# A two-layer spectral block on one core: channel-major filter temporaries, a regrouped prologue, reordered seams around the MLP, and products on constants in TensorE's waits

## The chip, the core and the metric

The kernel runs on one core of one Trainium2 chip. The metric is the device time of one execution in microseconds (us), lower is better. TensorE (PE) multiplies, VectorE (DVE), ScalarE (ACT) and GpSimd (POOL) do the elementwise work, SyncE (SP) issues nearly all transfers. All data are float32.

## What is computed

Two layers act on x of shape 2 x 128 x 128 x 128 (image, height, width, channel). Each layer does:

```python
residual = x
h = layer_norm(x, n1_g, n1_b)
h = afno_filter(h, w1, b1, w2, b2) + residual
residual = h
h = layer_norm(h, n2_g, n2_b)
h = gelu(h @ mw1 + mb1)       # exact, 128 -> 512
return h @ mw2 + mb2 + residual
# afno_filter(x):
xf = rfft2(x, norm='ortho')                    # over height and width
o1 = relu(block_diagonal(xf, w1) + b1)         # complex, 8 blocks of 16 channels
o2 = softshrink(block_diagonal(o1, w2) + b2, 0.01)
return irfft2(o2, norm='ortho') + x
```

## The kernel before

**Steps and stages.** A step is one layer on one image, four in all (`STEPS`, step 2 is the change of layer). A tile is four image rows, there are 32. On the partitions lies the width (or, inside the transform, a frequency or a channel pair). Each step has these stages, in the order of the main loop of TensorE (L686 to L693):
- `dft_w` (L486): the transform along the width, 32 groups of four channels, products at L496. ScalarE and VectorE evict alternate groups to SBUF (`a_out`, the copy at L336).
- `filter_` (L554): 34 units, 32 of them for four frequencies of one half of the channels, two small ones for the last frequency. For a unit: transform along the height (`dft_h`, L506), copy by ScalarE (`g_copy`, L708), first block product (`mix1`, L521/L523), `e_copy` by ScalarE, two combining operations of VectorE (`combine`, L931 and L932), `o_relu` by ScalarE (L722), second block product (`mix2`, L550), and on VectorE `shrink`: v = product + bias (L942), cl = clamp(v) (L944), v - cl written into the arena (L959). TensorE takes the units staggered: `dft_h(n+2)`, `mix1(n+1)`, `mix2(n)`. v and cl lie frequency-major; the arena wants the frequencies of a channel side by side, so L959 writes with 128 words from one channel to the next, channel innermost.
- `idft_h` (L581): the inverse along the height, 32 groups of four channels at L590, evicted alternately by ScalarE and VectorE (`evict_v`, L363).
- `mlp` (L646): the inverse along the width for two tiles at a time (first pair L654, others `idft_w`, L607 and L613), sums with the residual on VectorE (`h2`, L1007 to L1018), layer norm statistics (L879) and the inverse deviation in twelve small operations (`inverse_std`, L313 to L322, and L1127), normalizing on ScalarE (L737), transposes on TensorE (`turn`, L621), splitting of the tile in a high and a low part (L745 on ScalarE, `lower`, L1024, on VectorE), `fc1` (L632 to L634), gelu (L751), `fc2` (L641), and the new x on VectorE (`x_new`, L1038, `last_tile`, L1047), which SyncE stores.

**The next image beside the MLP.** While TensorE does the MLP of one step, the other engines prepare the next: SyncE loads `xnext`, VectorE takes its statistics, GpSimd normalizes four rows a tile into the other arena (`z_rows`, L1191; these are the scalings), multiplies the result by the gain (L1160), adds `mb2` to the residual of the current step (L1198) and adds xnext (L1164), and SyncE puts the sum `aside` in DRAM until the next step reads it. The next `dft_w` waits for all 32 tiles of `z_new`.

**The prologue of step 0.** It does that job with nothing beside it: four loads of 8 tiles, for each batch statistics and inverse deviation on VectorE (L879 to L899), and then scalings by ScalarE (22 of 32 tiles, L762) and VectorE (10 tiles, L904), gain product and residual on GpSimd (24 tiles, L1160 and L1164 of the loop at L1168) as soon as a tile is normalized, and on VectorE (8 tiles, L921 and L923, between the evictions of dft_w). The filter of step 0 overwrites the first 13 tiles of `first`, so ScalarE waits for their stores (`early_st`, L778).

**Weights of a layer.** `build_spectral` (L846) masks the block weights into dense matrices by 24 products of VectorE (L862), waits for two small products of TensorE (`dc_bias`, L475, L482), and scales (L871). For layer 1 it runs at the end of step 1's MLP, and `dc_bias(1)` stands before `dft_w(2)` in TensorE's queue. `split_weights` (L987) splits `mw1` in two parts after the first pair.

All waits are on semaphores by hand; an engine executes its queue in order, so an instruction that waits holds all behind it.

## Time and profile before

| quantity | us |
|---|---|
| median of 3 runs | 1789.91 |
| lowest and highest | 1786.05, 1791.61 |
| the profiled execution | 1787.48 |
| its span (first to last instruction) | 1785.7 |

| engine | busy us | share of the span |
|---|---|---|
| TensorE products | 1636.1 | 92% |
| TensorE weight loads (beside products) | 1453.6 | 81% |
| VectorE | 1195.5 | 67% |
| ScalarE | 934.6 | 52% |
| GpSimd | 630.5 | 35% |

The mean granted TensorE clock is 0.977 of full speed. A busy share is an average over stages: which engine ends a stage last has to be read stage by stage. All further times of a row are us from the start of the span, durations in us unless ns is said.

### The profile page before, as it was taken

To read this page: it belongs to the slowest core of one execution; us is meant where nothing else is said; L and a number is where in the kernel's file an instruction comes from. 1 tells how busy PE (TensorE), PEld (TensorE's weight loads), DVE (VectorE), ACT (ScalarE), POOL (GpSimd) and SP (SyncE) were. 2 spreads that over 40 slices of the span, in tenths; PEclk is the share of its full clock that TensorE was granted. 3 is DMA by queue.
4 is the path that set the end of the run, shared out by engine and by line. 5 is a ranking of instruction groups with operands and counts; after the bars stand their busy time and mean duration, and the time that the engine had idled before them with its cause. 6 is when DMAs were issued, how large, how long until landed. Compare 5 with 4: busy or idle time off the path is not lost.

```text
span 1785.7 us, 35087 instructions
## 1 busy us (share of the span) xinstructions
PE 1636.1 (92%) x11184; PEld 1453.6 (81%) x11184; DVE 1195.5 (67%) x2880; ACT 934.6 (52%) x1778; POOL 630.5 (35%) x756
## 2 busy tenths in 40 slices
PE   0099989999999998999999998999999999899999
PEld 0088878888889887888889887888888988688888
DVE  7959956666646976666664895666664697566663
ACT  4335426666634534666652452666663453466665
POOL 4800004777750001677781000477775000111111
PEclk9999989999998998999998999999999999999999
DMA  8210061333320033333330006133332003211111
GB/s 246 100 54 1 1 220 59 101 105 105 100 80 1 1 115 117 103 103 106 106 101 24 1 1 220 54 97 103 106 107 84 1 1 126 77 36 31 34 36 48
DMA packets 164896, 138.85 MB, mean 78 GB/s; under 512 B 9186, under 2 KB 127332, under 8 KB 164804
## 3 DMA queue, kind: packets, MB, share of 16 engines
q1 hardware_dynamic: 164516, 137.15, 24.0%
q8 instruction: 58, 0.95, 0.2%
q10 hardware_dynamic: 288, 0.46, 0.1%
q14 instruction: 34, 0.28, 0.0%
HBM read 70.47 MB, written 67.11 MB: 77 GB/s over the span
## 4 chain that ended last, share of the span: by engine, by line
PE 44%; DVE 21%; POOL 17%; issue 15%; ACT 1%; DVEq 1%; DMA 1%; SPq 0%; POOLq 0%; ACTq 0%
PE ps L641 13%; PE ps L496 7%; PE ps L590 6%; POOL arena L1191 6%; POOL gz L1160 4%; DVE vsb L942 4%; POOL gz L1164 4%; PE ps L632 4%; PE ps L634 3%; PE ps L633 3%; DVE csb L944 3%; DVE usb L931 3%; DVE usb L932 2%; POOL arena L1198 2%; PE ps L621 2%
## 5 line engine op out<-in xcount | busy, mean ns | idle before, releaser
L641 PEld LDWEIGHTS ps<-mw,gel 128*128 128x128 f32 x4096 | 533.2, 191 | 43.3
L641 PE MATMUL ps<-mw,gel 128*128 128x128 f32 x4096 | 536.4, 274 | 0.0
L751 ACT ACTIVATE gel<-ps,mb1f 128x512 f32<-128x512 f32 x512 | 351.6, 687 | 269.9 <-PE ps L634 238.7
L1198 POOL TENSOR_TENSOR arena<-arena,mb2rep 128x512 f32<-128x512 f32 x128 | 163.5, 1277 | 886.0 <-ACT hn L737 886.0
L632 PE MATMUL ps<-hth,mw1h 128*128 128x512 f32 x512 | 262.9, 513 | 8.1 <-DVE htl L1024 7.8
L1191 POOL TENSOR_SCALAR arena<-xnext,rstd,shift 128x128 f32<-128x128 f32 x384 | 168.4, 457 | 217.7 <-DVE shift L1127 217.7
L737 ACT ACTIVATE hn<-arena,shift,rstd 128x128 f32 (+1 forms) x512 | 221.6, 482 | 35.6 <-DVE shift L1127 35.6
L1007 DVE TENSOR_TENSOR arena<-ps,arena 128x512 f32 (+1 forms) x64 | 44.2, 691 | 266.0 <-PE ps L613 241.9
L496 PE MATMUL ps<-cst,arena 128*128 128x128 f32 x1024 | 130.2, 294 | 90.3 <-DVE arena L904 81.4
L634 PE MATMUL ps<-hth,mw1l 128*128 128x512 f32 x512 | 204.4, 399 | 0.0
L496 PEld LDWEIGHTS ps<-cst,arena 128*128 128x128 f32 x1024 | 129.4, 208 | 90.8 <-DVE arena L904 81.5
L633 PE MATMUL ps<-htl,mw1h 128*128 128x512 f32 x512 | 203.2, 397 | 0.0
L722 ACT ACTIVATE osb<-usb,vectors 128x512 f32<-128x512 f32 (+1 forms) x136 | 95.6, 703 | 172.2 <-DVE usb L932 172.2
L550 PEld LDWEIGHTS ps<-w2s,osb 128*128 128x128 f32 x1040 | 131.2, 195 | 46.0 <-ACT osb L722 44.0
L550 PE MATMUL ps<-w2s,osb 128*128 128x128 f32 x1040 | 153.9, 291 | 11.8 <-ACT osb L722 11.2
L959 DVE TENSOR_TENSOR arena<-vsb,csb 128x512 f32 (+2 forms) x128 | 133.6, 1044 | 15.4 <-DVE csb L944 0.2
L506 PE MATMUL ps<-cst,arena 128*128 128x128 f32 x1024 | 138.9, 280 | 0.3
L506 PEld LDWEIGHTS ps<-cst,arena 128*128 128x128 f32 x1024 | 128.3, 196 | 1.2 <-issue 0.8
L1160 POOL TENSOR_TENSOR gz<-arena,gain 128x512 f32<-128x512 f32 x96 | 124.6, 1298 | 8.0
L1024 DVE TENSOR_TENSOR htl<-ps,hth 128x512 fp32r<-128x512 f32 x128 | 88.2, 689 | 57.0 <-ACT hth L745 56.9
L1164 POOL TENSOR_TENSOR gz<-xnext,gz 128x512 f32<-128x512 f32 x96 | 122.4, 1275 | 0.5
L632 PEld LDWEIGHTS ps<-hth,mw1h 128*128 128x128 f32 x512 | 99.5, 194 | 24.3 <-issue 21.2
(92 smaller groups left out, 2428.8 us busy)
## 6 DMA issues: line engine op xcount, KB each, us to landing
arena<-aside SPq DMA_DIRECT2D x128, 256.0 KB, 5.0
aside<-gz SPq DMA_DIRECT2D x96, 256.0 KB, 3.0
between<-xout SPq DMA_DIRECT2D x62, 256.0 KB, 2.3
xnext<-between SPq DMA_DIRECT2D x62, 256.0 KB, 3.0
out_dram<-xout SPq DMA_DIRECT2D x62, 256.0 KB, 2.3
aside<-first SPq DMA_DIRECT2D x32, 256.0 KB, 2.0
xnext<-in_x_dram SPq DMA_DIRECT2D x31, 256.0 KB, 3.0
mw1raw<-in_L_mw_dram SPq DMA_DIRECT2D x4, 256.0 KB, 2.5
```

Of the source, the lines that this page charges most:

```text
L496: mm = pe.matmul(ps[:, 2 + cg % 4, P * i:P * i + P], rows_of(s)[:, (GROUP * cg + i) // 2, :, i % 2], FW, start=True, stop=True)
L506: mm = pe.matmul(ps[:, q, P * i:P * i + P], spec_of(s)[:, GROUP * b + i, q].rearrange("p r c -> p (r c)"), FH, start=True, stop=True)
L550: mm = pe.matmul(ps[:, 4 + q, P * i:P * i + P], osb[:, q, i, :], w2s[:, q].rearrange("p r c -> p (r c)"), start=True, stop=True)
L632: pe.matmul(bank, h, hth[:, r % 2, :], start=True, stop=False)
L633: pe.matmul(bank, h, htl[:, r % 2, :], start=False, stop=False)
L634: pe.matmul(bank, l, hth[:, r % 2, :], start=False, stop=True).then_inc(f1_mm, 1)
L641: mm = pe.matmul(ps[:, r % 2, P * i:P * i + P], gel[:, r % 2, m, P * i:P * i + P], mw2[:, m, :], start=(m == 0 and i == 0), stop=(m == CHU ...
L737: ins = act.activation(hn[:, r % 2, i, :], row, ACT.Identity, bias=shift[:, r // 2, r % 2 * ROWS + i:r % 2 * ROWS + i + 1], scale=rstd[:, ...
L751: act.activation(gel[:, r % 2, m, :], ps[:, 2 + m % 2], ACT.Gelu, bias=mb1f[:, m:m + 1]).then_inc(gelu_out, 1)
L1160: pool.tensor_tensor(by_row(tmp), ztile(s, h0), gains(gain1[:, :]), ALU.mult).then_inc(gz_done, 1)
L1191: ins = pool.tensor_scalar(zrow(s + 1, h0 + k), pairs(xnext[:, r, k, :]), rstd[:, r // 2, row:row + 1], shift[:, r // 2, row:row + 1], ALU ...
L1198: pool.tensor_tensor(t, t, b, ALU.add).then_inc(mb2_done, 1)
```

## The change

In the prologue the batches are 4, 8, 8, 8 and 4 tiles, the first load stands before the parameter loads, GpSimd takes part in the scalings (15 tiles, ScalarE 15, VectorE 2), and all gain products and residuals follow the last scaling: 12 tiles on GpSimd, 20 on VectorE with their temporaries in PSUM. ScalarE evicts all of dft_w of step 0. The building of the weights is moved behind the first batch, and for layer 1 between the evictions of dft_w of step 2; `dc_bias(1)` follows that dft_w. The filter's temporaries are channel-major. The last four groups of idft_h are evicted by ScalarE; the first pair's inverse along the width is done in two pieces, channels 0 to 95 inside idft_h and the rest after it, its sums likewise, and `split_weights` is done within idft_h. TensorE runs 14 and 5 products of two constant matrices, whose result nobody reads, before and after the first transposes. At the end of the MLP VectorE takes the last statistics before an earlier `x_new`, and GpSimd does the last scalings before the gain products.

```diff
-PRO_ACT = (7, 6, 6, 3)
+BATCH = (4, 8, 8, 8, 4)
+PRO_POOL = (2, 4, 4, 4, 1)
+PRO_ACT = (2, 4, 4, 4, 1)
-R_DVE = 8
+R_DVE = 20
+PARTS = 12
+SOON = 24
+V_DVE = SOON // 2 + 2
+V_ACT = CGROUPS - V_DVE
-Z_DVE0 = TILES - sum(PRO_ACT)
+Z_DVE0 = TILES - sum(PRO_ACT) - sum(PRO_POOL)
...
+        b2cols = sb("b2cols", [P, 2, HALF, 2])
-        vsb = at("vsb", [P, 2, GROUP, 2, HALF], o); o += size(vsb.shape)
-        csb = at("csb", [P, 2, GROUP, 2, HALF], o); o += size(csb.shape)
+        vsb = at("vsb", [P, 2, HALF, GROUP, 2], o); o += size(vsb.shape)
+        csb = at("csb", [P, 2, HALF, GROUP, 2], o); o += size(csb.shape)
...
+            for b in range(len(BATCH)):
+                lo, hi = at_row[b], at_row[b + 1]
+                if lo <= HALF < hi:
+                    load_first(b, lo, HALF - lo, lo + 1)
+                    sp.dma_start(first[:, HALF, :], source[0][0]).then_inc(row0_in, 16)
+                    load_first(b, HALF + 1, hi - HALF - 1, HALF + 1)
+                else:
+                    load_first(b, lo, hi - lo, lo + (lo < HALF))
+                if b == 0:
+                    load_spectral(0)
+                    load_gain(0)
...
-            for t in range(TILES):
+            turns = sorted(range(TILES), key=lambda t: 2 * t + 1 if t < R_POOL0 else t - R_POOL0)
+            for t in turns:
...
                     for r in range(4):
                         store(TILES // 4 - 1, r)
+                    for r in range(4):
                         put_aside(s, TILES // 4 - 1, r)
...
+            def first_pair(s, a, b):
+                if a == 0:
+                    pe.wait_ge(h2_done, TILES * s)
+                for cg in (b - 2, b - 1):
+                    turned(s, cg)
+                t = slice(GROUP // 2 * a, GROUP // 2 * b)
+                for bank, m, h0 in ((6, DE, 0), (7, DO, H - ROWS)):
+                    dst = ps[:, bank - (2 if a else 0), 0:ROWS * GROUP * (b - a)]
+                    mm = pe.matmul(dst, m, v_of(s)[:, t, h0:h0 + ROWS, :], start=True, stop=True)
+                mm.then_inc(iw_soon if a == 0 else iw_mm, 1)
...
                     mm.then_inc(ih_mm, 1)
+                    if cg == SOON + 1:
+                        first_pair(s, 0, SOON)
...
+            def keep_warm(n):
+                for _ in range(n):
+                    pe.matmul(ps[:, 2, 0:P], IDENT, FH, start=True, stop=True)
+
             def mlp(s):
-                pe.wait_ge(h2_done, TILES * s)
-                for half in range(2):
...
+                turned(s, SOON + 3)
+                first_pair(s, SOON, CGROUPS)
                 mlp_bias(s)
                 idft_w(s, 1)
+                keep_warm(14)
                 turn(s, 0, 0)
+                keep_warm(5)
                 pe.wait_ge(mlp_w, s + 1)
...
-                if s % IMAGES == 0:
+                if s == 0:
+                    dc_bias(0)
+                dft_w(s)
+                if s and s % IMAGES == 0:
                     dc_bias(s // IMAGES)
-                dft_w(s)
...
-                        for r in (0, 2):
+                        for r in ((0, 2) if s else range(4)):
                             a_out(s, q, j, r)
...
-                with act.Fori(0, CGROUPS // 4) as j:
+                with act.Fori(0, SOON // 4) as j:
                     for r in (0, 2):
                         v_out_(s, 4 * j + r, r)
+                for cg in (SOON, SOON + 2, *range(SOON + 4, CGROUPS)):
+                    v_out_(s, cg, cg % 4)
...
+                if b == 0:
+                    build_spectral(0)
+                if b == 1:
+                    scale_spectral(0)
+                for t in range(t0 + PRO_POOL[b], t0 + BATCH[b] - PRO_ACT[b]):
...
-                own.add(dve.tensor_tensor(by_row(gz0[:, :, :]), ztile(0, ROWS * t), gains(gain1[:, :]), ALU.mult))
+                tmp = ps[:, 6].rearrange("p (h c) -> p h c", h=ROWS)
+                own.add(dve.tensor_tensor(by_row(tmp), ztile(0, ROWS * t), gains(ps[:, 7, C:2 * C]), ALU.mult))
                 own.settle()
-                dve.tensor_tensor(first[:, h, :], first[:, h, :], gz0[:, :, :], ALU.add).then_inc(r_dve, 1)
+                dve.tensor_tensor(first[:, h, :], first[:, h, :], tmp, ALU.add).then_inc(r_dve, 1)
...
-                bias = b2rep[:, q].rearrange("p r c -> p (r c)").unsqueeze(1).to_broadcast([P, kws, P])
-                v = vsb[:, q].rearrange("p j r c -> p j (r c)")[:, 0:kws]
-                cl = csb[:, q].rearrange("p j r c -> p j (r c)")[:, 0:kws]
-                src = ps[:, 4 + q, 0:P * kws].rearrange("p (j k) -> p j k", j=kws)
+                bias = b2cols[:, q].unsqueeze(2).to_broadcast([P, HALF, kws, 2])
+                v, cl = vsb[:, q, :, 0:kws], csb[:, q, :, 0:kws]
+                src = ps[:, 4 + q, 0:P * kws].rearrange("p (j r c) -> p c j r", j=kws, r=2)
                 dve.tensor_tensor(v, src, bias, ALU.add).then_inc(v_out, 1)
...
-                dst = dst.rearrange("p c k -> p k c")
-                v, cl = (t.rearrange("p j r c -> p (j r) c") for t in (v, cl))
+                v, cl = (t.rearrange("p c j r -> p c (j r)") for t in (v, cl))
                 dve.tensor_tensor(dst, v, cl, ALU.subtract).then_inc(y_done, 1)
...
+                elif s % IMAGES:
...
+                else:
+                    dve.wait_ge(spec_in, SPEC_IN * (s // IMAGES + 1))
+                    for cg in range(1, CGROUPS, 2):
+                        a_out(s, 2 * cg // CGROUPS, cg % (CGROUPS // 2) // 4, cg % 4)
+                        if cg // 2 < PARTS:
+                            build_part(cg // 2)
+                        if cg // 2 == PARTS:
+                            build_done()
+                    scale_spectral(s // IMAGES)
...
+                split_weights(s)
+                dve.wait_ge(resid_in[0], RESID_IN[0] * (s + 1))
+                v_out_(s, SOON + 1, 1)
+                dve.wait_ge(iw_soon, s + 1)
+                h2_evens(s, 0, SOON)
+                v_out_(s, SOON + 3, 3)
+                own.settle()
+                h2_odds(s, 0, SOON)
+                own.settle()
...
-                    if known >= 3:
+                    if 3 <= known <= PAIRS or last and known > PAIRS:
                         x_new(s, i + (2 * h - 5) // 4, (2 * h - 5) % 4)
...
+                    if known > PAIRS and not last:
+                        x_new(s, i + (2 * h - 5) // 4, (2 * h - 5) % 4)
...
+            for b in range(len(BATCH)):
+                pool.wait_ge(st_pro, b + 1)
+                for t in range(sum(BATCH[:b]), sum(BATCH[:b]) + PRO_POOL[b]):
...
+                j = TILES // 4 - 1
+                if not last:
+                    ready(j, 0)
+                    z_rows(j, 0)
+                    z_rows(j, 1)
+                for n in (TILES - 2, TILES - 1):
+                    biased(n)
+                if not last:
+                    ready(j, 2)
+                    z_rows(j, 2)
+                    z_rows(j, 3)
+                    scaled(j, 0)
```

`turned(s, cg)` and `evicted(s, cg)` are waits for the eviction of group cg, by the engine that now does it; `h2_evens` and `h2_odds` are the two halves of `h2` on a range of channels; `ready`, `scaled`, `added`, `biased` are GpSimd's old pieces (wait for the statistics, gain product, residual, mb2).

## Rows read from the trace of the kernel before

**Rows 1.** Busy time per stage; columns: stretch, its length, the engines' busy time (instructions), granted clock, DMA.
```profile
core 0: us, PE busy (x) PEld busy (x) DVE busy (x) ACT busy (x) POOL busy (x), PEclk, DMA share, GB/s
0.00:91.90 91.90, 0.98 (x5) 0.92 (x5) 81.03 (x182) 35.59 (x89) 60.47 (x52) 1.00 0.54 168
...
126.00:223.40 97.40, 93.38 (x652) 82.06 (x653) 86.85 (x174) 49.75 (x102) 0.00 (x0) 0.99 0.02 6
223.40:252.80 29.40, 29.40 (x258) 29.40 (x257) 12.54 (x18) 9.30 (x16) 0.00 (x0) 0.97 0.89 308
252.80:272.40 19.60, 12.32 (x44) 7.98 (x44) 15.53 (x46) 8.27 (x17) 2.55 (x2) 0.74 0.12 40
272.40:509.60 237.20, 237.20 (x1573) 207.83 (x1571) 151.50 (x430) 148.67 (x274) 166.90 (x214) 1.00 0.32 98
```

**Rows 2.** Order of time, prologue; columns: start, duration, engine, line, output<-inputs, count, wait.
```profile
2.75 0.84 SPq L390 DMA_DIRECT2D first<-in_x_dram  x1
...
5.33 2.62 DVE L862 TENSOR_TENSOR w1s<-wraw,cst 64x64 f32<-64x64 f32 x16 [5.33 <-DMA betarow<-in_L_n_b_dram]
...
13.51 5.38 DVE L879 BATCH_NORM_STATS2 pst<-first 128x6 f32<-128x256 f32 x16 [1.82 <-DMA first<-in_x_dram]
...
21.67 10.89 ACT L762 ACTIVATE arena<-first,pnm,prs 128x128 f32<-128x128 f32 x28 [18.70 <-DVEq L900]
...
30.74 1.25 POOL L1160 TENSOR_TENSOR xout<-arena,gain 128x512 f32<-128x512 f32 x1
30.86 1.18 DVE L320 TENSOR_TENSOR pn<-pn,pva 128x32 f32<-128x32 f32 x1
```

**Rows 3.** Order of time, dft_w of step 0 and the first copy of its filter.
```profile
91.90 31.82 PEld L496 LDWEIGHTS ps<-cst,arena 128*128 128x128 f32 x256 [81.52 <-DVE arena L904]
...
123.94 0.69 DVE L336 COPY arena<-ps 128x512 f32<-128x512 f32 x1 [1.15 <-PE ps L496]
...
126.04 0.26 ACT L705 COPY nyq<-ps 64x128 f32<-64x128 f32 x1 [2.34 <-DVE first L923]
```

**Rows 4.** Groups by line and shape, filter of step 0 (150 to 214): busy us, mean ns.
```profile
L959 DVE TENSOR_TENSOR arena<-vsb,csb 128x512 f32 x23 | 24.4, 1060 | 3.3
...
L942 DVE TENSOR_TENSOR vsb<-ps,b2rep 128x512 f32<-128x512 f32 x23 | 15.7, 683 | 0.0
...
L944 DVE TENSOR_SCALAR csb<-vsb 128x512 f32<-128x512 f32 x23 | 9.8, 427 | 0.8
```

**Rows 5.** Order of time, filter of step 0: weight loads of dft_h, and L959.
```profile
146.61 0.97 PEld L506 LDWEIGHTS ps<-cst,arena 128*128 128x128 f32 x8
...
154.56 0.97 PEld L506 LDWEIGHTS ps<-cst,arena 128*128 128x128 f32 x8
...
182.40 1.05 DVE L959 TENSOR_TENSOR arena<-vsb,csb 128x512 f32 x1
...
216.40 1.06 DVE L959 TENSOR_TENSOR arena<-vsb,csb 128x512 f32 x1
```

**Rows 6.** Order of time, end of the MLP of step 0 and start of dft_w of step 1.
```profile
502.80 0.19 DVE L320 TENSOR_TENSOR nt<-nt,var 128x8 f32<-128x8 f32 x1
...
505.47 1.20 DVE L1127 SCALAR_TENSOR_TENSOR shift<-stats,rstd 128x8 f32<-128x8 f32 x1
...
512.26 1.74 POOL L1191 TENSOR_SCALAR arena<-xnext,rstd,shift 128x128 f32<-128x128 f32 x4
...
514.05 2.29 PE L496 MATMUL ps<-cst,arena 128*128 128x128 f32 x9 [4.43 <-POOL arena L1191]
```

**Rows 7.** Order of time, start of the MLP of step 0.
```profile
252.86 2.27 PE L654 MATMUL ps<-arena,cst 128*128 128x256 f32 x8
...
257.88 1.43 DVE L879 BATCH_NORM_STATS2 stats<-arena 128x6 f32<-128x256 f32 x4
...
263.46 1.12 PE L621 MATMUL ps<-cst,hn 128*128 128x128 f32 x4 [3.14 <-ACT hn L737]
...
266.24 0.77 PE L632 MATMUL ps<-hth,mw1h 128*128 128x512 f32 x1 [1.67 <-DVE htl L1024]
```

**Rows 8.** Order of time, TensorE between the MLP of step 1 and dft_w of step 2.
```profile
939.75 1.01 PE L482 MATMUL ps<-vectors,w1s 64*128 64x1 f32 x4 [4.94 <-DVEq L864]
```

More of the change, by code:

```diff
@@ L209, in afno @@
         nt0 = sb("nt0", [P, 4 * ROWS])
-        gz0 = sb("gz0", [P, ROWS, C])
         xout_at = top[0]
@@ L1221, in _, with ready, scaled @@
-                for n in range(TILES + 4):
-                    tile(n // 4, n % 4)
+                def ready(j, r):
+                    pool.wait_ge(rs_done, RS * s + 2 * (j + 1) + r // 2 + 1)
+                def scaled(j, r):
+                    m = 4 * j + r
+                    pool.wait_ge(z_new, TILES * s + m + 1)
+                    if s or m >= 4:
+                        pool.wait_ge(gz_st[r], 16 * (TILES // 4 * s + j))
+                    scale(s + 1, ROWS * tile_of(j, r), gz[:, r])
@@ new lines, in added, with biased @@
+                def added(j, r):
+                    pool.wait_ge(gz_done, R_POOL0 + TILES * s + 4 * j + r + 1)
+                    residual(gz[:, r], xnext[:, r], gz[:, r])
+                def biased(n):
+                    pool.wait_ge(hn_done, TILES * s + n + 1)
+                    bias(s, n // 4, n % 4)
+                for n in range(TILES):
+                    j, r = n // 4 - 1, n % 4
+                    if j >= 0 and not last:
+                        ready(j, r)
+                        z_rows(j, r)
+                        scaled(j, r)
+                    if n >= 2:
+                        biased(n - 2)
+                    if j >= 0 and not last:
+                        added(j, r)
```

207 lines of the change are left out of this document (109 added, 98 removed).

## Prediction

> **What bounds the kernel now.** I read the busy time by stage first, then the instructions in order of time at each seam between stages. One step (there are four, one per layer and image) is five stages: dft_w, filter, idft_h, the start of the MLP, the MLP. In the MLP TensorE is busy for all of its 237.20 us and in the filter for 93.38 of 97.40, with VectorE at 86.85 beside it; in the first 91.90 us TensorE does 0.98 us of work [rows 1]. So the change has to be read at three kinds of place: the prologue, where VectorE sets the pace; the filter, where two engines are close to each other; and the seams, where TensorE idles.
>
> The prologue's chain: statistics begin at 13.51, when the first load has landed; those of a batch of eight tiles take 5.38, and the twelve small operations of the inverse deviation take 2.78 when GpSimd is idle (18.89 to ScalarE's start at 21.67), so 0.23 each. Once GpSimd multiplies and adds, one of them takes 1.18, about as long as the GpSimd operation beside it (1.25) [rows 2]. dft_w starts at 91.90 and the filter's first copy at 126.04, after a wait of 2.34 for the last VectorE residual [rows 3].
>
> **Prologue.** After: batches of 4, 8, 8, 8, 4 tiles; GpSimd and ScalarE normalize 15 tiles each and VectorE two; all gain products and residuals come after the last normalized row. First load: half the bytes and first in its queue. Before, 2 MB took 10.76 from its issue at 2.75; half is 5.4, plus the issue and the constants that share the engines; I take 8.0 (bounds 6 and 10). VectorE then has 4 tiles of statistics 2.7 and 2.8 of small operations (13.5), the 24 products that build the weights (16 take 2.62, so 4.0, plus a copy 0.3: 17.8), then 8.2 for each of three batches (with 1.3 for scaling the weights in the first) to 43.7, 5.5 for the last to 49.2. I add 0.9 for the products that run beside GpSimd's scalings: 50.1. GpSimd normalizes a tile in 1.74 [rows 6]: four tiles from 44.6 end at 51.6, the last at 53.3. ScalarE takes 10.89/7 = 1.56 a tile [rows 2]: 44.6 + 6.2 + 1.6 = 52.4. VectorE's two tiles hide beside these. dft_w starts at 53.4: 38.5 earlier.
> What had been hidden under the prologue now lies beside dft_w, 31.8 long [rows 3]: GpSimd does 12 tiles of two operations, 12 x 2 x 1.3 = 31.2, ending at 84.6; the store of that tile has to land (about 2) before ScalarE may write over it, so 86.8. VectorE does 20 tiles of two operations with one operand in PSUM, 20 x 1.44 = 29, ending near 83 (nearest row the eviction L336 of the same size, 0.69 [rows 3]; a write to PSUM by VectorE is not in the trace; between 0.69 and the 1.06 of L959 [rows 4], with which it would be 37 and end at 91). ScalarE takes all 32 evictions: at 9.30/16 = 0.58 each [rows 1] they fit into 31.8. The filter's first copy comes at 86.8 against 126.04: I take a gain of 39 (bounds 34 and 42). If GpSimd blocked VectorE in its scalings as it does in its products, each small operation would take up to 1.74/4 = 0.44; the one row with a scaling beside it shows 0.19 [rows 6], so I don't charge it.
> The Trainium skill ("SBUF — State Buffer", the section on the bandwidth-pool intuition) says that GpSimd and a two-port VectorE operation exclude each other entirely. The products agree with it and the scalings do not; charged in full for the two batches whose small operations meet a scaling, twelve times 0.2 each, it is an estimate of 5 us more, 1712.
>
> **Filter.** The temporaries v and cl change from frequency-major to channel-major, so the last of the three operations of shrink (L959) writes runs of eight words instead of single words 512 B apart. It takes 1.060 now [rows 4] against 0.69 for the eviction L336, which writes 512 elements in runs of four [rows 3]; new value 0.69. The add (L942, 0.683 [rows 4]) now reads PSUM with a stride; L336 also does, 512 B from word to word, so I leave it (bounds 0.68 and 1.06). The clamp (L944, 0.427 [rows 4]) stays contiguous. VectorE's time per unit was (216.40 - 182.40)/12 = 2.83 [rows 5] and becomes 2.46. But TensorE needs (154.56 - 146.61)/3 = 2.65 per unit where it waits for nothing [rows 5]. So a unit gains 2.83 - 2.65 = 0.18 and no more. In step 0 TensorE's pace holds up to 154.56; from there to the last but two units before 216.40 [rows 5] there are (214 - 154.56)/2.83 = 21 units: 3.8. The last three units have less TensorE work and keep VectorE's whole 0.37: 1.1. Together, rounded, 5.0 per step, 20 for four (bounds 0 and 24).
>
> **Start of the MLP.** Three quarters of the first pair of row products move into idft_h: about 1.45 of TensorE time is spent earlier, and idft_h ends that much later. Against that, ScalarE evicts the last four column groups (0.58 each), and after the last there remain only products of 128 columns (0.45) and four short VectorE sums (1.2). Sum after the old end of idft_h: 1.45 + 0.75 + 0.45 + 0.2 + 1.3 = 4.15, against 257.88 - 252.86 = 5.0 before [rows 7]. The weight split moves into idft_h, where VectorE is busy for 12.54 of 29.40 [rows 1], so it is hidden there; without that cover it would cost its two operations of 512 elements, about 1.3. Queued behind the new wait for iw_soon are two evictions' worth of VectorE work; TensorE needs the first only four groups later. Then the chain statistics, normalize, transpose, copy, subtract. The transposes took 1.12 and fc1 started at 266.24 [rows 7]; the granted clock of this stretch is 0.74 [rows 1], so both levels, 1.2 and 2.4 GHz, occur in it, and TensorE had been waiting before each. The 14 + 5 products on constants take 29.40/128 = 0.23 each at the upper level [rows 1]: 3.2 after the second pair of row products, ending some 0.5 before the normalized tile is there, and 1.1 in the wait for htl. With TensorE at the upper level the transposes and the first fc1 group save 0.5 each, and VectorE's h2 no longer stands before the subtraction (0.2). In all 0.8 + 0.5 + 0.5 + 0.2 + 0.2 for later fc1 groups = 2.2 per step, 8.8 in all (bounds 2 and 12).
>
> **End of the MLP.** TensorE starts dft_w of step 1 at 514.05, after GpSimd's last scaling (512.26 + 1.74), and had waited 4.43, so it had finished at 509.62 [rows 6]. GpSimd now does the last two tiles' scalings before their gain products, and VectorE does the statistics before the x of an earlier tile. The statistics end by 504.9 instead of 506.67 (L1127 at 505.47 alone took 1.20 beside a product [rows 6]); then 2 x 1.75: 508.5. TensorE's own end is then last: gain 4.3 for steps 0 and 2. At the change of layer TensorE waited 4.94 for the built weights and with the bias products (1.01) began dft_w 5.8 after its MLP [rows 8]; the building moves between evictions, where VectorE waits 1.15 before each [rows 3], against two products of 0.16: 5.8. Total 14.4 (bounds 8 and 16). The x of tile 29 is now ready only 0.3 before fc2 of tile 31 asks for it; if it is later, it costs that. The bias product and the scaling of the weights now follow dft_w at that one place: 1.0 lost. Without the idle gap dft_w starts at the upper clock; its first groups of steps 1 to 3 ran below it: 2 gained (0 to 4).
> The DMAs that change place (the weights of step 0 behind the first batch, stores of step 0 in another order, the last asides behind the last x stores) stand behind nothing that is needed sooner: the last aside is read a whole dft_w later.
>
> **Sum.** 39 + 20 + 8.8 + 14.4 + 2 - 1 = 83.2. The profiled execution took 1787.5 (span 1785.7); its median is 2.4 more. 1787.5 - 83.2 = 1704.3, and 1706.7 in terms of the median.
>
> **Rivals.**
> (a) The filter gains nothing: L959 keeps 1.06 because the channels still lie 512 B apart. For it: no row has this mix of run and stride. Against: L336 [rows 3] also writes short runs, at 0.69. 1707 + 20 = 1727.
> (b) Slower than before: reading PSUM in channel order costs L942 what L959's writes cost now (0.38 more), the clamp falls to one element a cycle (0.27 more), and L959 doesn't gain. A unit is then 3.48, 128 units lose 83, the rest gains 63: 1787.5 + 20 + 2.4 = 1810. It decides from 0.49 more per unit (3.32) on. Against it is L336 at 0.69 with a strided read of PSUM [rows 3].
> The Trainium skill ("SBUF — State Buffer", the section on the DMA port swizzle) says that PSUM has lines of 8 bytes and that reads that are not contiguous are slow; it says so of matmuls. L336 shows no such price for VectorE; L959 shows one, for writes to SBUF.
> (c) The products on constants backfire: TensorE falls to the lower level anyway, 14 of them take twice as long, 6.4, and the transposes wait for them 2.9 longer than before, in four steps 11.5 lost instead of 8.8 gained: 1727.
> (d) The last scalings still come late (the statistics wait for GpSimd's biases or for the loads): half of the seams' gain goes, 1714.
> (e) The prologue is paced by something else (VectorE beside GpSimd's scalings, or the load): 5 to 6 us, 1712.
>
> **Chances.** Forecast 0.60; (a) 0.12; (b) 0.03; (c) 0.10; (d) 0.06; (e) 0.09. Range: the forecast's own bounds (filter +4, prologue +3, start +3, others +3 on the good side; as much again on the bad one) give 1692 to 1722; with (a) and (c) 1690 to 1730. A difference under 0.3% (5 us) can't be told from no change. Faster 0.96, same 0.01, slower 0.03.
>
> **What would show it.** dft_w starts at 53 (right: 51 to 57). L959's successor takes 0.69 and L942's 0.69; filter units follow each other at 2.65, and VectorE then waits, not TensorE. fc1 starts some 11.9 after the old end of idft_h (13.4 before) and its products are at the upper clock. TensorE's wait before dft_w is under 0.5. It would be wrong most by a filter unit at 2.83 or more, or by a first filter copy after 92.

## The result and the profile after

The changed kernel takes 1695.8 us (median of four, 1691.4 to 1697.6) against 1788.1 for the kernel before on the same chip: ratio 0.948, 95% interval 0.945 to 0.950. The forecast was 1706.7. The gain is 92 where the prediction had 83. The profiled execution took 1697.6 with a span of 1695.9 and a mean granted clock of 0.996 (0.977 before).

To see where the time went I lay the first instructions of the stages on TensorE side by side, each stage from its own first instruction to the first one of the next (us; worked out from the two traces):

| | before, step 0 | 1 | 2 | 3 | after, step 0 | 1 | 2 | 3 |
|---|---|---|---|---|---|---|---|---|
| start of dft_w | 91.9 | 514.1 | 940.7 | 1365.9 | 54.9 | 463.3 | 869.6 | 1285.8 |
| dft_w | 31.7 | 32.2 | 32.3 | 32.9 | 31.6 | 30.2 | **35.6** | 30.2 |
| filter | 99.6 | 102.9 | 102.9 | 98.4 | 93.7 | 93.0 | **96.6** | 93.0 |
| idft_h | 29.6 | 28.7 | 28.7 | 28.7 | 30.0 | 30.0 | 30.9 | 30.0 |
| its end to fc2 | 19.6 | 19.8 | 19.8 | 19.2 | 16.2 | 16.2 | 16.2 | 16.2 |
| MLP from fc2 on | 237.0 | 237.0 | 237.0 | 237.0 | 237.0 | 237.0 | 237.0 | 237.0 |
| idle until the next dft_w | 4.6 | 6.1 | 4.6 | | 0 | 0 | 0 | |

The differences: prologue 37.0, dft_w 1.7, filters 27.3, idft_h with the start of the MLP 8.3, idle at the seams 15.5: 89.8, the difference of the two spans. Step 1 of the changed kernel, which nothing disturbs, takes 406.3 to the next dft_w; step 2 is longer by 9.9, which the prediction had not foreseen.

**Prologue.** The changed kernel in order of time, the lines that answer to [rows 2] and [rows 3]:

```profile
8.61 2.73 DVE L943 BATCH_NORM_STATS2 pst<-first 128x6 f32<-128x256 f32 x8 [8.61 <-DMA first<-in_x_dram]
...
43.06 0.38 DVE L326 TENSOR_TENSOR pn<-prs 128x32 f32<-128x32 f32 x1
43.48 0.38 DVE L328 TENSOR_TENSOR pn<-pn,pva 128x32 f32<-128x32 f32 x1
43.89 0.19 DVE L330 SCALAR_TENSOR_TENSOR prs<-pn,prs 128x32 f32<-128x32 f32 x1
...
45.77 9.06 POOL L1280 TENSOR_SCALAR arena<-first,prs,pnm 128x128 f32<-128x128 f32 x20 [1.52 <-DVE pnm L961]
...
54.94 1.36 PEld L524 LDWEIGHTS ps<-cst,arena 128*128 128x128 f32 x6 [35.29 <-issue]
...
88.46 0.26 ACT L757 COPY nyq<-ps 64x128 f32<-64x128 f32 x1 [0.94 <-DMA aside<-first]
```

The first load landed at 8.61. A small operation of VectorE beside a scaling of GpSimd mostly takes 0.17 to 0.20, now and then 0.25 to 0.49 (0.38 at 43.06), against 1.18 beside a gain product before. GpSimd's last five tiles end at 54.83 and release dft_w. The filter's first copy waits 0.94 for a store to land, no longer for VectorE.

**Filter.** The groups by line and shape in the filter of step 0 (110 to 174), which answer to [rows 4]; and one round of weight loads, which answers to [rows 5]:

```profile
L1011 DVE TENSOR_TENSOR vsb<-ps,b2cols 128x512 f32<-128x512 f32 x25 | 17.1, 682 | 0.0
L1026 DVE TENSOR_TENSOR arena<-vsb,csb 128x512 f32 x24 | 16.6, 693 | 3.4
L1013 DVE TENSOR_SCALAR csb<-vsb 128x512 f32<-128x512 f32 x25 | 10.7, 427 | 0.9
```
```profile
130.19 0.97 PEld L534 LDWEIGHTS ps<-cst,arena 128*128 128x128 f32 x8
...
132.84 0.97 PEld L534 LDWEIGHTS ps<-cst,arena 128*128 128x128 f32 x8
```

The write into the arena (L1026, the former L959) takes 693 ns instead of 1060, the add that now reads PSUM with a stride stays at 682, the clamp at 427. A unit follows every 2.65, TensorE's own pace.

**Start of the MLP.** TensorE in step 0, in order of time (compare [rows 7]):

```profile
214.41 0.19 PEld L700 LDWEIGHTS ps<-cst 128*128 128x128 f32 x1 [0.24 <-issue]
214.84 3.09 PEld L700 LDWEIGHTS ps<-cst 128*128 128x128 f32 x27 [0.24 <-issue]
218.63 0.42 PEld L672 LDWEIGHTS ps<-cst,hn 128*128 128x128 f32 x4 [0.69 <-ACT hn L789]
219.02 1.20 PEld L700 LDWEIGHTS ps<-cst 128*128 128x128 f32 x10
220.75 0.19 PEld L683 LDWEIGHTS ps<-hth,mw1h 128*128 128x128 f32 x1 [0.54 <-issue]
```

A product on constants appears as two rows, so 14 are 28. They end 0.69 before the normalized tile is there. fc1 comes 10.6 after the end of idft_h, which itself is 1.3 longer: 11.9 after the old end.

**Seams.** GpSimd and TensorE at the end of step 0, which answer to [rows 6]:

```profile
458.82 3.48 POOL L1307 TENSOR_SCALAR arena<-xnext,rstd,shift 128x128 f32<-128x128 f32 x8 [2.15 <-DVE shift L1238]
462.26 2.53 POOL L1269 TENSOR_TENSOR gz<-arena,gain 128x512 f32<-128x512 f32 x2
```
```profile
460.83 2.73 PE L692 MATMUL ps<-mw,gel 128*128 128x128 f32 x23
463.40 2.87 PE L524 MATMUL ps<-cst,arena 128*128 128x128 f32 x23
```

The last scaling ends at 462.30, one microsecond before TensorE wants it, and dft_w follows the MLP without a gap.

**The clock.** Busy time of stretches; columns: stretch, length, the engines' busy time (instructions), granted clock, DMA share, GB/s. The first two are of the kernel before (filters of steps 1 and 2), the next two of the changed kernel:

```profile
552.90:563.10 10.20, 10.20 (x43) 9.32 (x42) 6.05 (x17) 3.12 (x7) 0.00 (x0) 0.50 0.00 0
979.50:989.80 10.30, 10.30 (x43) 9.43 (x43) 6.12 (x17) 3.12 (x7) 0.00 (x0) 0.50 0.01 2
```
```profile
493.40:586.50 93.10, 90.85 (x672) 85.21 (x671) 81.51 (x175) 53.06 (x103) 0.00 (x0) 1.00 0.00 1
616.40:632.60 16.20, 12.55 (x78) 10.03 (x78) 12.27 (x43) 8.39 (x17) 2.57 (x2) 1.00 0.24 89
```

Before, TensorE ran at the lower of its levels (0.50 of full speed) for a part of every step, 82 us in all; after, only in three stretches of step 2, 13.7 us together. The start of the MLP is at 1.00 where it was at 0.74 [rows 1].

**The stall in step 2.** Between the evictions of this dft_w stand VectorE's products for the new layer's weights. VectorE, GpSimd and TensorE of the changed kernel:

```profile
872.48 6.20 DVE L919 TENSOR_TENSOR w1s<-wraw,cst 64x64 f32<-64x64 f32 x2
878.61 0.67 DVE L344 COPY arena<-ps 128x512 f32<-128x512 f32 x1
879.21 0.34 DVE L919 TENSOR_TENSOR w1s<-wraw,cst 64x64 f32<-64x64 f32 x2
```
```profile
872.27 1.27 POOL L1269 TENSOR_TENSOR gz<-arena,gain 128x512 f32<-128x512 f32 x1
873.50 1.27 POOL L1273 TENSOR_TENSOR gz<-xnext,gz 128x512 f32<-128x512 f32 x1
874.73 1.29 POOL L1269 TENSOR_TENSOR gz<-arena,gain 128x512 f32<-128x512 f32 x1
875.97 2.49 POOL L1273 TENSOR_TENSOR gz<-xnext,gz 128x512 f32<-128x512 f32 x2
```
```profile
879.34 5.92 PE L524 MATMUL ps<-cst,arena 128*128 128x128 f32 x35 [2.89 <-DVE arena L344]
```

Two products that take 0.34 elsewhere take 6.20, beside the last five operations of an unbroken run of two-operand operations on GpSimd: they end 0.2 after that run (878.46). An eviction stands behind them, and TensorE waits 2.89 for it.

### The profile page after: what moved, and what is told of

Same layout as the page of the kernel before. It is cut to its first block, busy times and chain, and to the rows that moved or that the text cites. A ratio compares the mean times of both kernels' runs of the same rounds, so it can differ in the third digit from the quotient of the medians.

```text
span 1695.9 us, 35295 instructions
## 1 busy us (share of the span) xinstructions
PE 1611.5 (95%) x11336; PEld 1458.9 (86%) x11336; DVE 1136.1 (67%) x2879; ACT 949.7 (56%) x1774; POOL 628.3 (37%) x792
## 4 chain that ended last, share of the span: by engine, by line
PE 88%; DVE 4%; POOL 2%; ACT 2%; issue 1%; DMA 0%; DVEq 0%; ACTq 0%
PE ps L692 27%; PE ps L683 7%; PE ps L685 7%; PE ps L639 7%; PE ps L684 7%; PE ps L578 7%; PE ps L534 6%; PE ps L524 5%; PE ps L549 3%; PE ps L672 3%; PE ps L551 3%; PE ps L658 3%; PE ps L664 3%; POOL first L1273 1%; POOL xout L1269 1%; DVE stats L943 1%
## 5 line engine op out<-in xcount | busy, mean ns | idle before, releaser
L524 PE MATMUL ps<-cst,arena 128*128 128x128 f32 x1024 | 124.6, 286 | 38.1 <-POOL arena L1280 35.2
L524 PEld LDWEIGHTS ps<-cst,arena 128*128 128x128 f32 x1024 | 124.0, 200 | 38.4 <-issue 35.3
L578 PEld LDWEIGHTS ps<-w2s,osb 128*128 128x128 f32 x1040 | 137.4, 194 | 18.9 <-ACT osb L774 13.2
L578 PE MATMUL ps<-w2s,osb 128*128 128x128 f32 x1040 | 142.9, 280 | 8.5 <-ACT osb L774 7.9
L534 PE MATMUL ps<-cst,arena 128*128 128x128 f32 x1024 | 136.2, 276 | 0.2
L534 PEld LDWEIGHTS ps<-cst,arena 128*128 128x128 f32 x1024 | 125.7, 193 | 0.9 <-issue 0.5
L797 ACT CAST hth<-ps 128x512 fp32r<-128x512 f32 x128 | 75.2, 588 | 79.7 <-PE ps L672 79.7
```

Of the source, the lines that this page charges most:

```text
L524: mm = pe.matmul(ps[:, 2 + cg % 4, P * i:P * i + P], rows_of(s)[:, (GROUP * cg + i) // 2, :, i % 2], FW, start=True, stop=True)
L534: mm = pe.matmul(ps[:, q, P * i:P * i + P], spec_of(s)[:, GROUP * b + i, q].rearrange("p r c -> p (r c)"), FH, start=True, stop=True)
L578: mm = pe.matmul(ps[:, 4 + q, P * i:P * i + P], osb[:, q, i, :], w2s[:, q].rearrange("p r c -> p (r c)"), start=True, stop=True)
```

## The experiments

Each ran with the kernel before beside it on the same chip. A change of a few microseconds is read from the stages of the trace, since executions of one kernel differ by up to 11 with the share of time at the lower clock: the changed kernel took 1691.5 where its mean granted clock was 1.000, and 1697.9 where it was 0.995. "Longer than the changed kernel" is said against its first median, 1695.8; the medians of the kernel before lay between 1785.4 and 1788.6 in these groups of runs, so a few microseconds of such a difference mean nothing.

**The layout by itself, taken away and added.** First the changed kernel with the old order of v and cl:

```diff
-        vsb = at("vsb", [P, 2, HALF, GROUP, 2], o); o += size(vsb.shape)
-        csb = at("csb", [P, 2, HALF, GROUP, 2], o); o += size(csb.shape)
+        vsb = at("vsb", [P, 2, GROUP, 2, HALF], o); o += size(vsb.shape)
+        csb = at("csb", [P, 2, GROUP, 2, HALF], o); o += size(csb.shape)
...
-                v, cl = (t.rearrange("p c j r -> p c (j r)") for t in (v, cl))
+                dst = dst.rearrange("p c k -> p k c")
+                v, cl = (t.rearrange("p j r c -> p (j r) c") for t in (v, cl))
```

> The changed kernel with the filter's temporaries frequency-major again; everything else stays. Theory (VectorE paces the old filter at 2.83 us a unit, TensorE the new one at 2.65): units come 2.83 apart again, the last operation of shrink takes 1.06 again, each of the four filters is 5 to 6 us longer, and the kernel takes 1696 + 22 = 1718. Rival (the layout is worth all that the filter stages gained between the two kernels, 27 us): 1723 or more. Rival (the layout is worth nothing, the filters gained by the seams alone): 1696.

1720.9 (1715.0 to 1725.7), ratio to before 0.962 [0.959, 0.966]: 25 longer than the changed kernel, between the 1718 of the theory and the 1723 of the first rival. The filters of steps 1 to 3 take 98.30 each, where an undisturbed one of the changed kernel takes 93.03, 5.3 a filter or 21 in all; the last operation is back at its old time:

```profile
L1029 DVE TENSOR_TENSOR arena<-vsb,csb 128x512 f32 x19 | 20.1, 1060 | 2.7
```

Then the kernel before with the channel-major layout and nothing else of the change (the bias copied once into that order; the buffer gz0 gave way to a temporary in PSUM):

> The kernel before with channel-major temporaries and the transposed copy of the bias, nothing else of the change (to make room in SBUF the eight residual temporaries of VectorE lie in PSUM, as in the changed kernel). Theory: units 2.65 apart, each filter 5 to 6 us shorter, 1788 - 22 = 1766; the stretches at the lower clock at the start of the filters of steps 1 and 2 stay, because the idle gap before dft_w stays. Rival (the layout is worth 27 us): 1761. Rival (VectorE was not the pace of the old filter): 1788.

1766.1 (1763.9 to 1771.6), ratio 0.988 [0.985, 0.991]: 21.6 shorter than before. The operation takes 693 ns here too, a filter 93.0 where no stretch at the lower clock falls into it (step 2) and up to 97.7 where one does (step 3). So the layout is worth 21 by its units and 22 to 25 in the medians whatever stands around it, and rival (a) is out. One part of the expectation failed: the idle time before dft_w stayed, but the stretches at the lower clock did not stay at the start of the filters of steps 1 and 2; the one of 10 us lay at the start of step 3's.

**Which engine paces the filter.** The changed kernel with the clamp done twice (the last two lines of the edit count the added operation):

```diff
-                own.add(dve.tensor_scalar(cl, v, -LAM, LAM, ALU.max, ALU.min))
-                own.settle()
+                for _ in range(2):
+                    own.add(dve.tensor_scalar(cl, v, -LAM, LAM, ALU.max, ALU.min))
+                    own.settle()
...
-                    own.enter(b, 2, 2)
+                    own.enter(b, 4, 2)
```

> The changed kernel with the clamp of each filter unit done twice (the same result): 0.43 us more on VectorE in each of the 32 large units. Theory: TensorE sets the pace of 2.65 us per unit, VectorE needs 2.46 and has 0.19 to spare; the unit becomes 2.46 + 0.43 = 2.89 and each filter 24 to 30 units x 0.24 = 6 to 8 longer, 24 to 30 in all: 1720 to 1726. Rival V (VectorE already paced the filter at 2.65): the unit becomes 3.08, 52 in all, 1748. Rival N (there is more slack than the sum of the rows says): unchanged.

1743.8 (1742.2 to 1746.1): 48 longer than the changed kernel (49 by its second run, on the same chip), 104.3 a filter. The time is nearer to rival V than to the theory, so I read the unit itself, VectorE in order of time:

```profile
120.08 0.41 DVE L1002 TENSOR_TENSOR usb<-usb,ps 128x252 f32<-128x252 f32 x1
120.41 0.68 DVE L1011 TENSOR_TENSOR vsb<-ps,b2cols 128x512 f32<-128x512 f32 x1
121.13 0.89 DVE L1014 TENSOR_SCALAR csb<-vsb 128x512 f32<-128x512 f32 x2
122.16 0.69 DVE L1027 TENSOR_TENSOR arena<-vsb,csb 128x512 f32 x1
122.77 0.41 DVE L1001 TENSOR_TENSOR usb<-usb,ps 128x252 f32<-128x252 f32 x1
123.09 0.41 DVE L1002 TENSOR_TENSOR usb<-usb,ps 128x252 f32<-128x252 f32 x1
```

A unit is now 3.01 and VectorE never waits. The second clamp adds 0.46 (its 0.43 and 0.03 until it starts), so without it VectorE needs 3.01 - 0.46 = 2.55, not 2.46. TensorE still paces the changed filter at 2.65, but by 0.10 and not by 0.19. In the changed kernel itself the next operation starts 0.70 after L1026 does (129.31 to 130.01) where it starts 0.61 after it here (122.16 to 122.77): a wait of 0.09, which agrees. Most of the 0.09 that the forecast of 2.46 lacked was lost in the way durations were subtracted: that distance was 0.90 in the kernel before (154.06 to 154.96), a saving of 0.29, while the printed durations differ by 0.37.

**The prologue: which of its edits carries it.** The kernel before with one wait moved:

```diff
-            done = [0, 0]
+            pool.wait_ge(z_dve, Z_DVE0)
+            pool.wait_ge(z_act, sum(PRO_ACT))
             for t in range(R_POOL0):
-                who = 0 if t % PB < PB - PRO_ACT[t // PB] else 1
-                done[who] += 1
-                pool.wait_ge((z_dve, z_act)[who], done[who])
```

> The kernel before with one wait moved: GpSimd begins its gain products of the prologue only after the last scaling of VectorE and ScalarE. Nothing else of the change. Theory L (the prologue was long because GpSimd's two-operand operations hold up VectorE's, 1.18 instead of 0.19 for a small operation and 8.06 for two tiles of scalings instead of 2.26): VectorE's chain is then 22.9, twice 10.4, and 5.4 + 2.8 + 5.7 for the last batch, and dft_w starts at 57.6 instead of 91.9. GpSimd's 24 tiles then last to 119 and give a part back: the first copy of the filter at 95 instead of 126, and up to 10 lost by VectorE in the filter beside GpSimd. Time 1762 (1755 to 1770). Rival (the chain was long for its own work or the loads): dft_w starts after 85 and the time is 1780 to 1800, since the products come later for nothing.

1792.0 (1788.5 to 1796.1), ratio 1.002 [1.001, 1.003]: nothing gained, and the time is the rival's. The trace shows that the theory's mechanism was there and its consequence was not. VectorE, TensorE, GpSimd and ScalarE, in order of time:

```profile
39.12 0.19 DVE L320 TENSOR_TENSOR pn<-pn,pva 128x32 f32<-128x32 f32 x1
41.27 2.15 DVE L904 TENSOR_SCALAR arena<-first,pst,prs 128x128 f32<-128x128 f32 x8
```
```profile
56.84 5.41 PEld L496 LDWEIGHTS ps<-cst,arena 128*128 128x128 f32 x25 [46.55 <-DVE arena L904]
```
```profile
124.15 1.26 POOL L1164 TENSOR_TENSOR first<-first,xout 128x512 f32<-128x512 f32 x1
```
```profile
125.44 0.26 ACT L705 COPY nyq<-ps 64x128 f32<-64x128 f32 x1 [35.05 <-POOL first L1164]
```

No operation of VectorE is held up before dft_w, which starts at 56.84 (57.6 expected, 91.9 before). But the first copy of the filter comes at 125.44, where it had been at 126.04. I had let it wait for the first 13 tiles; the code waits for all 24 residuals of GpSimd. What the chain gained, the queue of products gave back.

So the other half had to be tried, the changed kernel with GpSimd keeping 24 of these tiles:

```diff
-R_DVE = 20
+R_DVE = 8
```

> The changed kernel with the split of the gain products and residuals of the prologue as before: 24 tiles on GpSimd and 8 on VectorE, instead of 12 and 20. The scalings still come first. Theory C (the prologue's gain needs both edits: scalings first, and half of GpSimd's products given to VectorE): dft_w still starts at 54 to 55, but ScalarE's first filter copy waits for GpSimd's 24 tiles at 2.55 to 2.86 each, that is until 116 to 124 instead of 88; with a stretch at the lower clock after that wait the time is 1724 to 1736. Rival (the split is a detail): under 10 longer than the changed kernel, below 1706.

1729.8 (1728.8 to 1731.6), 34 longer than the changed kernel. dft_w starts at 54.2 and the copy waits:

```profile
116.12 0.26 ACT L757 COPY nyq<-ps 64x128 f32<-64x128 f32 x1 [28.71 <-POOL first L1273]
```

Of the 34, 27.7 are this wait (116.12 against 88.46); the filter behind it starts at the lower clock (0.92 from 118 to 220). The two edits are complements: alone the first is worth nothing, and without the second the changed kernel loses 34. Not tried by themselves: the second edit in the kernel before, the batches of 4 and 8 tiles, and the first load at the head of its queue.

The third part, GpSimd's share in the scalings:

```diff
-PRO_POOL = (2, 4, 4, 4, 1)
-PRO_ACT = (2, 4, 4, 4, 1)
+PRO_POOL = (0, 0, 0, 0, 0)
+PRO_ACT = (3, 6, 6, 6, 2)
```

> The changed kernel with GpSimd's 15 scalings of the prologue given to ScalarE (23 tiles) and VectorE (9). Theory: VectorE's chain gets 7.9 longer (seven tiles of 1.13) less some 0.9 that GpSimd's scalings cost its small operations; the last batch but one is ready at 50.9 instead of 45.8, ScalarE's six tiles of it (9.4) and two of the last (3.1) end at 63.4, and dft_w starts there, 8.5 to 9 later than in the changed kernel: 1703 to 1706. Rival (GpSimd's scalings cost VectorE what they spare it): dft_w starts before 57, 1694 to 1698.

1703.5 (1700.9 to 1708.6), 8 longer. dft_w starts at 61.2 (ScalarE's last scaling ends at 61.15), 6.3 later than in the changed kernel; 8.5 had been expected. GpSimd's scalings are worth their place, though rival (e) had a grain of truth: without them the small operations of VectorE all take 0.19.

**The seams.** The changed kernel with the old order of the last tiles on GpSimd and VectorE:

```diff
...
-                    if known > PAIRS and not last:
-                        x_new(s, i + (2 * h - 5) // 4, (2 * h - 5) % 4)
...
-                for n in range(TILES):
+                for n in range(TILES + 4):
...
-                if not last:
-                    ready(j, 0)
-                    z_rows(j, 0)
-                    z_rows(j, 1)
...
```

> The changed kernel with the old order at the end of the MLP: GpSimd does each tile's gain product before the next tile's scaling, and VectorE writes the x of an earlier tile before the last statistics. Theory: TensorE waits 4.3 to 4.9 for the last scalings at each of the three seams (14 together), and the lower clock comes back at the start of dft_w or of the filter behind them (2 to 4): span 16 to 18 longer, 1712 to 1714. Rival (the order isn't what closed the seams, but something earlier in the MLP): under 5 longer, 1696 to 1701.

1712.6 (1711.8 to 1715.5), 17 longer. The idle time is back at all three seams (5.1 each), and the dft_w behind them take 31.5 to 32.7, where that of step 1 in the changed kernel takes 30.15:

```profile
468.59 1.75 POOL L1305 TENSOR_SCALAR arena<-xnext,rstd,shift 128x128 f32<-128x128 f32 x4
```
```profile
470.39 3.87 PE L524 MATMUL ps<-cst,arena 128*128 128x128 f32 x19 [5.11 <-POOL arena L1305]
```

The stall of step 2 is gone in this run: only two of GpSimd's products stand behind the last scaling, they end at 886.1, and VectorE's first product for the weights comes at 887.71 and takes 0.34 with its neighbour. The new order at the seams and the new place of the weight products make the stall between them.

**The products on constants.** The changed kernel without its two `keep_warm` calls:

> The changed kernel without the 14 and 5 products on constants. Theory: TensorE idles for 3 us before the first transposes and falls to the lower clock around fc1 in each step, as before the change: from the end of idft_h to the first fc2 it takes 1.0 to 2.0 us more than 16.2, in four steps 4 to 8, so 1700 to 1704. Rival (the closed gaps alone keep the upper clock, the products are idle work): 1696, with the granted clock at 1.0 in that stretch. Rival (the products held the transposes up): 1690.

1699.1 (1697.7 to 1700.4), 3.3 longer, just under the 1700 expected; the intervals of the two ratios overlap (0.950 [0.948, 0.952] against 0.948 [0.945, 0.950]), so the gain is read from the stage. The start of the MLP takes 16.7 to 17.4 instead of 16.2, its granted clock is 0.80 instead of 1.00 (stretch of step 1), and 41 us of the kernel lie at the lower clock instead of 13.7. By the stage they pay 3.0 in four steps, where the prediction had 4 (1.0 a step).

**The weights of the new layer.** The changed kernel with their products begun ten evictions later, two parts at a time, when GpSimd has done its run:

```diff
-                        if cg // 2 < PARTS:
-                            build_part(cg // 2)
-                        if cg // 2 == PARTS:
+                        part = 2 * (cg // 2 - 5)
+                        if 0 <= part < PARTS:
+                            build_part(part)
+                            build_part(part + 1)
+                        if part == PARTS:
```

> The changed kernel with the weights of layer 1 built from the sixth eviction of VectorE in dft_w of step 2 on, two parts per eviction, instead of from the first on, one part each: none of the products then runs beside GpSimd's last gain products and residuals. Theory (a VectorE product with two operands in SBUF is kept out while GpSimd's two-operand operations follow each other without a gap: 6.07 us for one product at 872.5; TensorE then waits 2.9 for evictions and falls to the lower clock): dft_w of step 2 takes 30.2 to 31.2 instead of 35.6, the stretches at the lower clock in step 2 are gone, in all 6 to 9 us: 1688 to 1690. Rival (building between evictions is what costs, wherever it stands): 35 again for dft_w of step 2 and 1696.

1696.8 (two others 1693.4 and 1696.7; a fourth execution took 3368.6, which nothing on record explains and which is left out): the same as the changed kernel, not the 1688 to 1690 expected. The stall is gone, four products in 0.62:

```profile
891.48 0.62 DVE L919 TENSOR_TENSOR w1s<-wraw,cst 64x64 f32<-64x64 f32 x4
```

dft_w of step 2 takes 30.9 instead of 35.6 and its filter 93.0 instead of 96.6, 8.3 gained. They are lost again elsewhere: 20.5 us at the lower clock lie in the other three steps, a stretch of 3.4 in each on the constant products. TensorE in step 0:

```profile
215.63 0.33 PEld L700 LDWEIGHTS ps<-cst 128*128 128x128 f32 x1 [0.52 <-issue]
216.48 3.94 PEld L700 LDWEIGHTS ps<-cst 128*128 128x128 f32 x27 [0.52 <-issue]
220.34 0.47 PEld L672 LDWEIGHTS ps<-cst,hn 128*128 128x128 f32 x4
```

The transposes no longer wait for the tile but for the products; the stage is 17.2, as if it had none. This is rival (c) in small: 1.0 a step. So the stage shows what made the stall, and no gain in the whole time came of its removal.

To see whether the stall was an accident I ran the changed kernel a second time:

> The changed kernel, without an edit, a second time. Theory S (the stall in the change of layer is built in: while the weight products stand between the evictions, one VectorE product meets GpSimd's run of two-operand operations in every execution): dft_w of step 2 is again longer than that of steps 1 and 3 (35.57 against 30.15 in the first profile), by 3 to 6 us, and the time is 1695 to 1697. Theory R (it was an accident of one execution): dft_w of step 2 is within 1 us of the others and the profiled span is 1686 to 1691.

1694.7 (1691.5 to 1697.9); dft_w of step 2 took 35.49, with a wait of 2.81 for the same eviction. It is built in. Then both remedies together, the later weights and 9 products instead of 14:

> The changed kernel with the weight products of the new layer begun ten evictions later (as in the run of that name) and 9 instead of 14 products on constants before the first transposes. Theory: when a stretch at the lower clock falls on the 14 products, they last into the transposes and the stage loses 1.0 (17.2 instead of 16.2, three of the four steps there). With 9 the stretch from the end of idft_h to fc2 is 16.2 to 16.5 in all four steps, and the time is 2 to 4 us under that run's 1696.8: 1693 to 1695. Rival: the clock falls more often with fewer products (transposes and first fc1 at the lower level), the start is 16.7 to 17.4 and the time 1697 to 1699.

1695.7 (1689.5 to 1698.6). The start is 16.2 in all four steps although a stretch at the lower clock fell on the products of step 3 (its 18 rows ended before the tile came). The time is still that of the changed kernel within the scatter. The mechanism of the expectation held, its sum didn't show.

At last these two with one more tile of residuals on VectorE (`R_DVE = 21`):

> The changed kernel with three small edits: the new layer's weight products ten evictions later, 9 instead of 14 products on constants, and 21 instead of 20 tiles of the prologue's residuals on VectorE (GpSimd, whose last residual ends at 86.25 in the changed kernel, then ends 2.5 earlier). Theory: the first filter copy comes 0.8 earlier, dft_w of step 2 takes 31 instead of 35.5, and what stretches at the lower clock take elsewhere leaves 1 to 3 of it: 1692 to 1694. Rival K (the stretches at the lower clock take all of it again): 1695 to 1696, the same as the changed kernel.

1691.9 (1688.6 to 1697.7), ratio 0.949 [0.946, 0.951] against 0.950 [0.947, 0.952] for the changed kernel in its second run. The copy of the filter was not earlier (88.55 against 88.46). The profiled execution had no stretch at the lower clock before the last few microseconds and a span of 1686.9, with dft_w of step 2 at 30.9 and all filters at 93.0 to 93.3. Where both kernels ran at a mean clock of 1.000 they took 1688.7 and 1688.6 against 1691.4 and 1691.5: 2.8 shorter. In the medians it can't be told from the changed kernel.

## Why the prediction was right, and where it was not

- **Prologue** (39 forecast): dft_w at 54.9 against 53.4, filter copy at 88.5 against 86.8, so 37.6 instead of 39. The first load took 8.6 instead of 8.0; VectorE's small operations beside scalings took up to 0.49 now and then and 0.19 mostly, some 1.4 more in all (0.9 forecast), far from the 5 us of the estimate that charged every small operation in full; the last five scalings of GpSimd took 9.06 instead of 8.7. The reason given was right, and it needs both of its halves: the two one-sided runs show that moving the products alone brings nothing, and that with 24 tiles left to GpSimd 34 are lost. The copy was paced at 84.6 + 2 by GpSimd's residuals and their store in the forecast, and by that store in the trace.
- **Filter** (20, measured 27.3): the unit is 2.65 as forecast, L1026 0.69, L1011 0.68. Step 3, which had no lower clock in its filter before, gained 5.3, step 0 5.9. Steps 1 and 2 gained 9.8 and 6.3: before, 10 us of each ran at 0.50, and the sum had no term for it. The step that failed is the one that gave the clock 2 us, at dft_w alone.
- **VectorE's need per unit** was put at 2.46 and is 2.55. It changed nothing in the sum, since TensorE paces at 2.65, but the reserve is 0.10.
- **Start of the MLP** (8.8, measured 8.3): fc1 at 11.9 after the old end, as forecast. The products on constants end 0.69 before the tile (0.5 forecast) and are worth 3.0 (4 forecast).
- **Seams** (14.4, measured 15.5): statistics end 4.8 before TensorE's end (463.56; 4.7 forecast), the last scaling 1.3 before it (1.1 forecast). The run with the old order gives 17 with its dft_w.
- **Clock** (2): dft_w of step 1 gained 2.1 and that of step 3 2.8 by it, and dft_w of step 2 would have gained 2.1 (32.25 to 30.15) without the stall: 6.9. The filters' share is 9.6 (403.66 before, less 4 x 5.33 for the unit, less 93.68 and 3 x 93.03). So this term is 16.5 and was mis-sized by 14.5, the largest error of the sum. What took the stretches away from the filters of steps 1 and 2 is not shown: with the old order at the seams, with the old layout and without the products on constants, each taken away by itself, no stretch comes back at their start.
- **Not foreseen:** the stall of step 2. The prediction put two products of 0.16 against 1.15 of waiting and left out what runs beside them: GpSimd's postponed gain products, which the same change had moved to just this place. Of the 9.9 by which step 2 is longer, 0.7 is the bias product behind dft_w (30.88 in the run with later weights against 30.15), which the sum had at 1.0; the 9.2 left are the stall and the stretches at the lower clock in that step, which the sum had at nothing. That the stretches follow from the stall is not shown.

Together: 14.5 (clock), 1.3 (filter unit 5.33 instead of 5.0), 1.1 (seams) and 0.3 (bias product) more, 9.2 (stall), 1.4 (prologue) and 0.5 (start of the MLP) less make 6.1 of the 6.6 between 83.2 and 89.8. Two large errors of opposite sign stood behind a total that was 7 off: that it came so near is in part luck.

The range was not what its own terms give: 4, 3, 3 and 3 are 13 on either side of 1706.7, 1694 to 1720, where the prediction wrote 1692 to 1722. The 1695.8 lies in both.

Of the rivals, (a) is excluded by the rows and both layout runs, (b) by L1011 at 0.68, (d) by the seams, (e) by dft_w at 54.9. (c) did not occur in the first profile of the changed kernel, whose start of the MLP takes 16.2 in all four steps, but did where a stretch at the lower clock fell on the 14 products: in step 2 of its second profile and in three steps of the run with later weights (1.0 a step, not 2.9: the stretch there lasted 3.4, where the rival had all 14 products at the lower level, 6.4).

## What to carry to other kernels

Before a short VectorE operation is put into a gap of 1 us, look at what GpSimd does at that moment: the operation may last as long as GpSimd's run, as two of 0.17 each did here (6.20). When a chain is shortened by moving work behind it, find who waits for the moved work; here one edit without the other was worth nothing. Take an engine's time per round from start to start and not from the durations, and give the clock its own term in the sum where stretches of the stage ran below full speed.

## What the runs showed of the hardware

- GpSimd's operations on two tensors in SBUF can hold up a VectorE operation until their whole run ends, not only until the current one does: 6.12 and 6.20 for two products, across five GpSimd operations with no gap. In the prologue of the kernel before it was one operation at a time: small ones of VectorE took 1.14 to 1.25, and every second or third 0.18 or 0.19. What makes the difference is open. An operation of 8 columns took 2.63, beside two biases of GpSimd (2.51 together):

```profile
454.07 2.63 DVE L323 TENSOR_SCALAR rstd<-var 128x8 int32<-128x8 int32 x1
```

- Evictions from PSUM were not held up beside the same operations (0.67 to 0.69), nor was a sum with one operand in PSUM (L991 and L993 of the prologue, 0.69 to 0.70 beside GpSimd's products). With its temporary in SBUF instead the residual's add took 1.64 in the kernel with scalings first. That the temporary in PSUM is what makes the 20 tiles on VectorE cheap was not tried by itself.
- The Trainium skill ("SBUF — State Buffer", the section on the bandwidth-pool intuition) says that GpSimd and a two-port VectorE operation exclude each other entirely. The stall agrees with it in kind, and lasts over five of GpSimd's operations. GpSimd's scalings, which read one tensor, do not: they cost a small operation up to 0.3 at times and mostly nothing.
- A read of PSUM by VectorE in channel order (L1011) costs nothing (682 against 683 ns), while a write to SBUF whose words lie 512 B apart costs 0.37 for 512 columns (1060 against 693).
- Which stretches run at the lower clock differs from execution to execution of one kernel (13.7 us in step 2 in both profiles of the changed kernel, the last stretch at the end of the filter in one and at the start of the MLP in the other; none in two of its timed runs, where the mean clock was 1.000). Why removing the stall moved them to other steps is open.
